# A hybrid block's second stage on one Trainium2 core: the next chunk's products, convolution and delta moved into this chunk's scan loop

## Chip, cores and metric

One core of a Trainium2 chip. The metric is the device time of one launch in microseconds (us); the kernel before takes 3812.79 us, the median of 3 runs (3812.38 to 3813.08).

## The reference

Three blocks follow each other on `x` of 2 sequences x 2048 tokens x 512 channels, viewed as needed: (1) an RWKV attention block with a recurrence over time; (2) a feed-forward block, and a Mamba block around which it stands; all with LayerNorm ahead and a residual behind. What matters here is the Mamba block and the feed-forward block (gate, up and down weights gathered from a table of 16 values, `silu(gate) * up`, then down):

```python
proj = einsum('blh,eh->ble', hidden, in_proj_w)        # 512 -> x (1024) and gate (1024)
x, gate = proj[..., :1024], proj[..., 1024:]
u = silu(conv1d(x, 4 taps, causal, per channel) + conv_b)
ssm_p = einsum('bld,rd->blr', u, x_proj_w)             # 128 (low rank of delta) + 16 (B) + 16 (C)
delta = softplus(einsum('blr,dr->bld', dt_lr, dt_proj_w) + dt_proj_b)
def step(h, xs):                                       # 16 states per channel
    h = h * exp(d_t[..., None] * A) + (d_t * u_t)[..., None] * B_t[:, None, :]
    return h, einsum('bdn,bn->bd', h, C_t)
y = (scan(step) + u * D_param) * silu(gate)
return einsum('bld,hd->blh', y, out_proj_w)
```

## The kernel before

The 4096 tokens are cut into 16 chunks of 256 (`NC = 16`, `CH = 256`). A first stage (to about 731 us) does the RWKV block; the change leaves it alone. The second stage runs feed-forward and Mamba over the chunks. Everything is written out by hand per engine: each engine has its own `step(i)` for chunk i, and semaphores join them, so that an engine's order is the order of its code.

In `step(i)` there are two parts. A **head**, in which TensorE (PE) has already made x of chunk i in PSUM (`first_product`, two halves of four 128-channel tiles in `W[0]` and `W[1]`), ScalarE (ACT) copies it to SBUF with room for three older tokens (`xext`) and starts `U` (`taps`), VectorE (DVE) adds the three other taps (`conv`, L1259), ACT applies silu (`smooth`, L944), PE multiplies by `x_proj_w` (L1137 and L1141) and by `dt_proj_w` into the eight PSUM tiles `D` (L1147), and delta follows by pairs of tiles: `D + bias` capped (DVE L1285, "below"), exp and ln on ACT (`soft`, L970 and L972), the maximum (DVE L1292), and `U * delta` (DVE L1297). Then a **scan loop** of 64 steps, one per state n and pair j of tiles (e = 4n + j): ACT computes `exp(delta * A)` into the pair's tiles of `D` (L1007), GpSimd (POOL) `dBu = U*delta * B` (L866), DVE two scans over the 256 tokens in place in `D` (L1308) and the product with C (L1327 or L1330), and POOL (three pairs of four, L879) or DVE (the fourth, L1339) adds it into `yacc`. ACT's exponentials of step e wait until the product of step e-4 is there, since they overwrite its tiles.

Inside the loop, at steps given by `places`, ACT and DVE serve two feed-forward blocks that PE runs meanwhile: one of a chunk ahead (`early`, F1) and one of the chunk before (`late`, F2). Each is a LayerNorm (`stats` and `shift` on DVE, `norm` on ACT), a transpose on PE (`turn`), its copy to SBUF (`evac`), six pieces of gate and up products with silu (ACT) and `gated` (DVE), the down products (L1096), and a residual (`resid`). PE also multiplies the gate half of `in_proj_w` (L1159) and projects the finished chunk (`project`, L1114). `gate_y` (L1237) closes the chunk. `W[0]` and `W[1]` are the only PSUM besides `D`, and all of this shares them. ACT must hold the right function table: `ACT_TABLE_LOAD` stands in its stream wherever the next function needs another one.

## Time and profile before

| | |
|---|---|
| median of 3 runs | 3812.79 us |
| the profiled execution's own time | 3813.42 us |
| its span in the trace | 3811.6 us |
| granted TensorE clock, mean | 0.942 of full |
| busy share of the span | PE 87%, PEld 62%, DVE 86%, ACT 65%, POOL 64% |
| first stage, second stage | 0 to about 731 us, about 731 to 3811.6 us |

The span is the time from the first to the last instruction of the one profiled execution; its own time is 1.8 us longer, and the median of the runs is 0.6 us below that. PE is the matrix engine with PEld its weight loads, which overlap it. Busy shares are means over stages with different limits, so the chunks are read one by one in the trace. A float32 matmul is two instructions in the trace.

### The profile page before, as it was taken

The numbers are of one execution on the slowest core, as the hardware profiler recorded it, in microseconds if no ns is written. First come the engines' busy times: TensorE is split into PE (matmuls) and PEld (weight loads), VectorE is DVE, ScalarE is ACT, GpSimd is POOL, SyncE is SP. The second block draws the span as 40 slices with busy tenths as digits, with TensorE's granted clock in tenths as the row PEclk, the third lists the DMA queues.
The fourth block names the chain that finished last, engine by engine and source line by source line (L and its number), as shares of the span: only waits on it lengthen the run. The fifth ranks groups of instructions, "written<-read, shape, count | busy, mean of one in ns | idle before, by whom it ended". The sixth has DMA issues, their size and how long they took to land.

```text
span 3811.6 us, 46308 instructions
## 1 busy us (share of the span) xinstructions
PE 3318.6 (87%) x12672; PEld 2365.7 (62%) x12672; DVE 3286.4 (86%) x6128; ACT 2489.4 (65%) x4790; POOL 2454.7 (64%) x1943
## 2 busy tenths in 40 slices
PE   5888984999999999999999999999999999985738
PEld 4666662666767676767676767666666666663515
DVE  5888883299999998989898989898989898989891
ACT  4777672186767676767676858676767676765650
POOL 0344343086869595959595959595969595957470
PEclk8999997999999999999999999999999999987868
DMA  2222212111111111111111111111111111101010
GB/s 99 65 74 73 76 61 84 61 37 40 30 43 31 42 33 41 39 34 41 34 41 34 41 33 41 34 39 35 40 35 39 35 39 37 47 27 37 20 36 6
DMA packets 119378, 165.36 MB, mean 43 GB/s; under 512 B 8545, under 2 KB 84193, under 8 KB 118625
## 3 DMA queue, kind: packets, MB, share of 16 engines
q1 hardware_dynamic: 119136, 162.63, 15.2%
q8 instruction: 92, 1.51, 0.2%
q14 instruction: 150, 1.22, 0.1%
HBM read 128.39 MB, written 25.69 MB: 40 GB/s over the span
## 4 chain that ended last, share of the span: by engine, by line
POOL 28%; PE 20%; DVE 17%; issue 15%; ACT 2%; DVEq 1%; POOLq 0%; DMA 0%; SPq 0%; ACTq 0%
POOL dBu L866 16%; POOL yacc L879 12%; DVE D L1308 10%; PE W L1064 6%; PE W L1114 5%; PE W L1096 3%; PE W L1137 2%; DVE prod L1327 2%; PE W L1141 2%; DVE D L1330 2%; PE D L1064 1%; DVE U L1259 1%; DVE yacc L1339 1%; ACT L916 1%; DVE hT L1221 1%
## 5 line engine op out<-in xcount | busy, mean ns | idle before, releaser
L1308 DVE TENSOR_TENSOR_SCAN D<-D,hc,dBu 128x256 f32<-128x256 f32 x2048 | 1436.9, 740 | 47.0 <-ACT D L1007 47.0
L866 POOL TENSOR_TENSOR dBu<-U,BC 128x512 f32<-128x512 f32 x1024 | 1294.3, 1275 | 276.4 <-DMA BC<-bc_scratch 200.3
L1064 PE MATMUL W<-nT,wffn 128*128 128x256 f32 x5632 | 1241.6, 382 | 47.2 <-ACT nT L905 32.6
L1064 PEld LDWEIGHTS W<-nT,wffn 128*128 128x128 f32 x5632 | 1058.8, 189 | 230.6 <-ACT nT L905 37.5
L1007 ACT ACTIVATE D<-delta,A 128x256 f32<-128x256 f32 x2048 | 891.7, 468 | 425.7 <-DVE yacc L1339 404.8
L879 POOL TENSOR_TENSOR yacc<-yacc,prod 128x512 f32<-128x512 f32 x736 | 933.9, 1269 | 263.0 <-DVE prod L1327 258.5
L1096 PE MATMUL W<-wffn,hT 128*128 128x512 f32 (+1 forms) x1408 | 642.0, 613 | 41.5 <-DVE hT L1221 41.5
L1096 PEld LDWEIGHTS W<-wffn,hT 128*128 128x128 f32 (+1 forms) x1408 | 273.8, 197 | 373.4 <-issue 323.8
L1327 DVE TENSOR_TENSOR prod<-D,BC 128x512 f32<-128x512 f32 x736 | 494.6, 672 | 0.0
L1064 PE MATMUL W<-nT,win 128*128 128x256 f32 x2048 | 453.9, 383 | 33.7 <-ACT nT L905 33.7
L1064 PEld LDWEIGHTS W<-nT,win 128*128 128x128 f32 x2048 | 391.4, 192 | 106.4 <-ACT nT L905 44.9
L450 PE MATMUL rvkP<-xnT,wr 128*128 128x256 f32 x1536 | 348.8, 387 | 31.3 <-ACT kk L328 16.0
L450 PEld LDWEIGHTS rvkP<-xnT,wr 128*128 128x128 f32 x1536 | 296.7, 194 | 83.2 <-ACT kk L328 17.8
L1114 PE MATMUL W<-wo,sgm 128*128 128x512 f32 x512 | 229.4, 602 | 65.3 <-DVE sgm L1237 65.3
L1007 ACT ACT_TABLE_LOAD x212 | 272.0, 1283 | 3.8
L848 POOL TENSOR_TENSOR rstd<-veps,mhalf 128x2 f32<-128x2 f32 x48 | 33.6, 699 | 349.5 <-DVE veps L1207 349.5
L995 ACT ACTIVATE hc<-D 128x2 f32<-128x2 f32 x736 | 117.3, 159 | 191.2 <-DVE prod L1327 190.7
L916 ACT ACT_TABLE_LOAD x182 | 233.5, 1283 | 3.3
L429 PE MATMUL trP<-wo,yT 128*128 128x512 f32 x256 | 140.5, 711 | 90.1 <-POOL yT L272 55.5
L1114 PEld LDWEIGHTS W<-wo,sgm 128*128 128x128 f32 x512 | 97.0, 192 | 182.5 <-issue 181.8
L1221 DVE TENSOR_TENSOR hT<-nrm,W 128x512 f32<-128x512 f32 x192 | 121.5, 633 | 95.9 <-ACT nrm L916 95.9
L1339 DVE TENSOR_TENSOR yacc<-D,yacc 128x512 f32<-128x512 f32 x288 | 193.5, 672 | 2.3
(118 smaller groups left out, 3212.0 us busy)
## 6 DMA issues: line engine op xcount, KB each, us to landing
BC<-bc_scratch SPq DMA_DIRECT2D x256, 256.0 KB, 4.6
XM<-x_scratch SPq DMA_DIRECT2D x29, 512.0 KB, 4.9
X<-x_scratch SPq DMA_DIRECT2D x17, 512.0 KB, 3.6
ix<-idx SPq DMA_DIRECT2D x33, 255.0 KB, 2.9
X<-x SPq DMA_DIRECT2D x16, 512.0 KB, 3.4
XR<-x SPq DMA_DIRECT2D x16, 512.0 KB, 3.4
x_scratch<-XR SPq DMA_DIRECT2D x16, 512.0 KB, 3.7
out<-X SPq DMA_DIRECT2D x16, 512.0 KB, 2.8
```

Of the source, the lines that this page charges most:

```text
L450: last = T_.matmul(rvkP[u % 3][:, m % 2, :], wr[:, k, part * H + m * P:part * H + (m + 1) * P], xnT[sf][:, k, :], start=(k == 0), stop=(k ...
L866: nc.gpsimd.tensor_tensor(dBu[e % 4][:], U[:, 2 * j:2 * j + 2, :], BC[slot][:, 0:1, :].to_broadcast([P, 2, CH]), ALU.mult).then_inc(s_dBu, 1)
L879: nc.gpsimd.tensor_tensor(y, y, prod[r % 2][:], ALU.add).then_inc(s_acc, 1)
L916: N_.activation(nrm[0:r[0][1], p % 2, 0:w], W[(side + p) % 2][0:r[0][1], 0:len(r), :].rearrange("p a t -> p (a t)"), ACT.Silu).then_inc(f_ ...
L1007: N_.activation(D[:, m, :], delta[:, m, :], ACT.Exp, scale=A[:, m, n:n + 1]).then_inc(s_dA, 1)
L1064: last = T_.matmul(dst, lhsT, rhs, start=(n == 0), stop=(n == len(terms) - 1))
L1096: return T_.matmul(o[:, t, :], hT[0:r, k, t * P:(t + 1) * P], wd[0:r, k, :], start=(k == 0), stop=(k == MI - 1))
L1114: last = T_.matmul(o[:, t, :], sgm[:, k, t * P:(t + 1) * P], wo[:, k, :], start=(k == 0), stop=(k == ME - 1))
L1221: V.tensor_tensor(hT[0:n, 2 * p:2 * p + w, :], nrm[0:n, p % 2, 0:w * CH].rearrange("p (a t) -> p a t", a=w), W[(side + p) % 2][0:n, 2:2 + ...
L1308: V.tensor_tensor_scan(D[:, m, :], D[:, m, :], dBu[e % 4][:, m % 2, :], hc[:, n, m:m + 1], ALU.mult, ALU.add).then_inc(s_scan, 1)
L1327: V.tensor_tensor(prod[r % 2][:], h_, c_, ALU.mult).then_inc(s_prod, 1)
L1339: V.tensor_tensor(yacc[:, pair, :], D[:, pair, :], yacc[:, pair, :], ALU.add).then_inc(s_prod, 1)
```

## The change

A head no longer stands between two scan loops. While chunk i is scanned, x of chunk i+1 is made (`first`), its convolution (`conv`, now reading x directly out of PSUM `W`), silus and `x_proj` are done, and the last steps of the loop are mixed with chunk i+1's delta, pair by pair (`delta_proj`, `below`, `soft`, `to_delta`). So that x can be read in place, `xext` goes; the three first tokens of a tile get their missing taps from a small tensor `edge`, which POOL makes out of the last three tokens of the chunk before (`tail`). `U * delta` goes to a tensor of its own (`dU`), the transposed rows `nT` get two buffers, the output residual is done in two halves, the list of places is new, and the last two chunks also give POOL three of four sums. The explicit load of the table that holds both exp and ln (L960) is taken out. The normalised rows for `first` are made one chunk earlier, which saves one reload of a row buffer per chunk. The core of the difference:

```diff
-xext = [buf(ctx, f"xext{s}", [2, CH + KC - 1]) for s in range(2)]
-cc = buf(ctx, "cc", [ME, KC - 1])
+nT = [buf(ctx, f"nT{s}", [KH, CH]) for s in range(2)]
+dU = buf(ctx, "dU", [ME, CH])
+tail = buf(ctx, "tail", [ME, KC - 1])
+edge = buf(ctx, "edge", [ME, KC - 1])
+term = buf(ctx, "term", [ME, KC - 1])
...
+    if i + 2 < NC:
+        stat = [(norm_no(*early(i)), 1), (norm_no(*late(i)), 8), (norm_no("M", i + 2), 41)]
+        return dict(stat=stat, early=(1, 3), late=(8, 10), m=(NEVER, NEVER), m2=(41, 43), out=(4, 6),
+                    norm=5, gate=(9, 12), evac=18, silu=(21, 24, 27, 29, 32, 34), res=38,
+                    norm2=36, evac2=39, silu2=(44, 46, 49, 52, 54, 56), res2=NEVER, norm_m=NEVER, evac_m=NEVER, norm_m2=58, evac_m2=NEVER,
+                    taps=(14, 17), conv=(12, 14), smooth=(21, 21, 24, 24), low=61, bc=63)
...
-            pe.wait_ge(s_prod, NE * i)
-            pe.wait_ge(s_ha, pool_sums(i))
-            pe.wait_ge(m_dtl, i + 1)
-            for m in range(ME):
-                last = chain(D[:, m, :], [(wdt[:, m * P:(m + 1) * P], dtl[:])])
-                if m % 2:
-                    last.then_inc(m_dp, 1)
-            if back:
-                project(i - 1, 0, FILL)
-                project(i - 1, 1)
+        def delta_proj(k):
+            pe.wait_ge(m_dtl, k + 1)
+            for j in range(4):
+                if k:
+                    e = NE - 4 + j
+                    pe.wait_ge(s_prod, NE * (k - 1) + e + 1)
+                    pe.wait_ge(s_ha, pool_sums(k - 1) + upto(e + 1))
+                for m in (2 * j, 2 * j + 1):
+                    last = T_.matmul(D[:, m, :], wdt[:, m * P:(m + 1) * P], dtl[:], start=True, stop=True)
+                last.then_inc(m_dp, 1)
+            if low is not None:
+                x_proj(low, 1 - side)
+            for k in range(MI):
+                if k == TURN_AT and then is not None:
+                    if low is not None:
+                        pe.wait_ge(m_bcS, low + 1)
+                    turn(then, 1 - side)
+            for m in range(4):
+                last = gate(i, m)
+            last.then_inc(m_g, 1)
+            if i:
+                project(i - 1)
+            for m in range(4, ME):
+                if i and m % 2 == 0:
+                    pe.wait_ge(m_res, 2 * (i - 1) + m // 2 - 1)
+                last = gate(i, m)
+            last.then_inc(m_g, 1)
+            if i + 1 < NC:
+                pe.wait_ge(m_sg, 2 * i + 1)
+                first(i + 1, 0)
+                pe.wait_ge(m_sg, 2 * i + 2)
+                first(i + 1, 1)
+                pe.wait_ge(m_tail, 2 * i + 5)
+                free = (m_tail, 2 * i + 6)
+            if i + 2 < NC:
+                turn(norm_no(*early(i)), 0)
+                ffn(ffn_no(*early(i)), norm_no(*early(i)), i % 2, 0, free, L)
+                ffn(F, L, i % 2, 1, (f_res, F), norm_no("M", i + 2), i + 1)
+            if i + 1 < NC:
+                delta_proj(i + 1)
...
-                N_.activation(xext[q % 2][:, :, KC - 1:], src[:, a:a + 2, :], ACT.Copy).then_inc(m_ext, 1)
-                act.wait_ge(s_dBu, NE * i)
-            N_.preload_act_table_set("natural_log_exp_and_others")
-            skip(0)
-            skip(1)
-            soft(0)
-            soft(1)
+        def taps(k, q):
+            act.wait_ge(m_x, 2 * k + q // 2 + 1)
+            act.wait_ge(m_du, 4 * k)
+            for h in range(2):
+                m = 2 * q + h
+                N_.activation(U[:, m, :], W[q // 2][:, m % 4, :], ACT.Identity, bias=cb[:, m:m + 1],
+                              scale=cw[:, m, KC - 1:KC]).then_inc(m_tap, 1)
+        def smooth(k, q):
+            act.wait_ge(m_edge, 2 * k + q // 2 + 1)
+            N_.activation(U[:, 2 * q:2 * q + 2, :], U[:, 2 * q:2 * q + 2, :], ACT.Silu).then_inc(m_u, 1)
+                for m in (2 * j, 2 * j + 1):
+                    N_.activation(D[:, m, :], delta[:, m, :], ACT.Exp, scale=A[:, m, n:n + 1]).then_inc(s_dA, 1)
+                if e == 0:
+                    soft(i, 3)
+                if e < 4:
+                    skip(i, e)
+                    if i + 1 < NC and e == at["taps"][h]:
+                        taps(i + 1, 2 * h)
+                        taps(i + 1, 2 * h + 1)
+                if f1 and e == at["evac"]:
+                    evac(norm_no(*early(i)), i % 2, 0)
+                if i + 1 < NC and e == at["low"]:
+                    low_rank(i + 1, 1 - side_late(i))
+                if i + 1 < NC and e == at["bc"]:
+                    b_and_c(i + 1, 1 - side_late(i))
+            if 0 < i < NC - 2:
+                evac(norm_no("M", i + 2), i % 2, 0)
+            for j in range(4):
+                save(i, NE - 4 + j)
+                if i + 1 < NC and j < 3:
+                    soft(i + 1, j)
...
+        def edges(k):
+            pool.wait_ge(m_tail, 2 * k + 2)
+            pool.wait_ge(m_edge, 2 * k)
+            nc.gpsimd.tensor_tensor(edge[:], tail[:], cw[:, :, 0:1].to_broadcast([P, ME, KC - 1]), ALU.mult).then_inc(m_term, 1)
+            for d in (1, 2):
+                pool.wait_ge(m_term, 5 * k + 2 * d - 1)
+                w = KC - 1 - d
+                nc.gpsimd.tensor_tensor(term[:, :, 0:w], tail[:, :, d:KC - 1], cw[:, :, d:d + 1].to_broadcast([P, ME, w]),
+                                        ALU.mult).then_inc(m_term, 1)
+                pool.wait_ge(m_term, 5 * k + 2 * d)
+                nc.gpsimd.tensor_tensor(edge[:, :, 0:w], edge[:, :, 0:w], term[:, :, 0:w], ALU.add).then_inc(m_term, 1)
...
-            V.tensor_copy(x_[:, :, 0:KC - 1], cq).then_inc(m_in, 1)
-                    V.scalar_tensor_tensor(U[:, m, :], x_[:, h, k:k + CH], cw[:, m, k:k + 1], U[:, m, :],
-                                           ALU.mult, ALU.add).then_inc(m_conv, 1)
-            V.tensor_scalar(cq, x_[:, :, CH:CH + KC - 1], keep[:, bass.ds(i + 1, 1)], None, ALU.mult).then_inc(m_cc, 1)
+        def conv(k, q):
+            dve.wait_ge(m_tap, ME * k + 2 * q + 2)
+            for d in range(KC - 1):
+                for h in range(2):
+                    m = 2 * q + h
+                    if d:
+                        dve.wait_ge(m_conv, 24 * k + 6 * q + 2 * (d - 1) + h + 1)
+                    V.scalar_tensor_tensor(U[:, m, KC - 1 - d:CH], W[q // 2][:, m % 4, 0:CH - KC + 1 + d], cw[:, m, d:d + 1],
+                                           U[:, m, KC - 1 - d:CH], ALU.mult, ALU.add).then_inc(m_conv, 1)
+        def ends(k, h):
+            half = slice(4 * h, 4 * h + 4)
+            dve.wait_ge(m_term, 5 * (k + 1))
+            V.tensor_scalar(tail[:, half, :], W[h][:, :, CH - KC + 1:CH], keep[:, k + 1:k + 2], None, ALU.mult).then_inc(m_tail, 1)
+            dve.wait_ge(m_conv, 24 * k + 12 * (h + 1))
+            V.tensor_tensor(U[:, half, 0:KC - 1], U[:, half, 0:KC - 1], edge[:, half, :], ALU.add).then_inc(m_edge, 1)
...
-            V.tensor_scalar(hc[:], hc[:], keep[:, bass.ds(i, 1)], None, ALU.mult).then_inc(s_hz, 1)
-            dve.wait_ge(s_scan, 2 * NE * i)
+        def below(k, j):
+            if k:
+                dve.wait_ge(s_scan, 2 * NE * (k - 1) + 2 * (NE - 3 + j))
+        def to_delta(k, j):
+            pair = slice(2 * j, 2 * j + 2)
+            V.tensor_tensor(dU[:, pair, :], U[:, pair, :], delta[:, pair, :], ALU.mult).then_inc(m_du, 1)
+                if e == 1:
+                    to_delta(i, 3)
+                if i and more and e >= NE - 2 and e <= NE:
+                    below(i + 1, e - NE + 2)
+                if i and more and e >= NE:
+                    to_delta(i + 1, e - NE)
+                for h in range(2):
+                    if more and e == at["conv"][h]:
+                        conv(i + 1, 2 * h)
+                        conv(i + 1, 2 * h + 1)
+                        ends(i + 1, h)
+            gate_y(i)
+            if more:
+                to_delta(i + 1, 2)
+                below(i + 1, 3)
```

Three places in the order of the instructions. First VectorE, end of the scan loop and start of the next chunk's (chunk 1 to 2; `D` holds first the delta projection, then the scan's factors and states). Before, the whole head stands between two loops:

```order
L1279 TENSOR_SCALAR hc<-hc,keep 128x128
L1285 TENSOR_SCALAR dBu<-D,bdt 128x256 x8
L1292 SCALAR_TENSOR_TENSOR delta<-D,bdt,dBu 128x256 x2
L1297 TENSOR_TENSOR U<-U,delta 128x512
L1292 SCALAR_TENSOR_TENSOR delta<-D,bdt,dBu 128x256 x2
L1297 TENSOR_TENSOR U<-U,delta 128x512
```

After (a scan is printed as SCALAR_TENSOR_TENSOR):

```order
L1331 SCALAR_TENSOR_TENSOR D<-D,hc,dBu 128x256 x2
L1351 TENSOR_TENSOR prod<-D,BC 128x512
L1312 TENSOR_SCALAR dBu<-D,bdt 128x256 x2
L1331 SCALAR_TENSOR_TENSOR D<-D,hc,dBu 128x256 x2
L1351 TENSOR_TENSOR prod<-D,BC 128x512
L1312 TENSOR_SCALAR dBu<-D,bdt 128x256 x2
L1339 COPY hc<-D 128x2
L1354 TENSOR_TENSOR D<-D,BC 128x512
L1312 TENSOR_SCALAR dBu<-D,bdt 128x256 x2
L1321 SCALAR_TENSOR_TENSOR delta<-D,bdt,dBu 128x256 x2
L1324 TENSOR_TENSOR dU<-U,delta 128x512
```

One block of eight has become three pairs that alternate with the last scans. Second ScalarE at the same place, where delta's exp (L970) and ln (L972) stand. Before:

```order
L960 ACT_TABLE_LOAD
L965 ACTIVATE yacc<-U,dsk 128x256 x4
L970 ACTIVATE dBu<-dBu 128x512
L972 ACTIVATE dBu<-dBu 128x512
L970 ACTIVATE dBu<-dBu 128x512
L972 ACTIVATE dBu<-dBu 128x512
```

After (L964 is the exp, L966 the ln, L973 the copy that saves a pair's last state):

```order
L906 ACTIVATE nT<-W 128x1024
L973 ACTIVATE hc<-D 128x2
L964 ACTIVATE dBu<-dBu 128x512
L966 ACT_TABLE_LOAD
L966 ACTIVATE dBu<-dBu 128x512
L973 ACTIVATE hc<-D 128x2
L964 ACT_TABLE_LOAD
L964 ACTIVATE dBu<-dBu 128x512
L966 ACT_TABLE_LOAD
L966 ACTIVATE dBu<-dBu 128x512
L973 ACTIVATE hc<-D 128x2
```

Every change between exp and ln now has a load of its own, and each save stands behind the exp and ln of the pair before. Third TensorE over one chunk, from the end of the second feed-forward block to the middle of the next. Before:

```order
L1064 MATMUL W<-nT,win 128x256 x32
L1137 MATMUL W<-U,wx 128x256 x2
L1141 MATMUL W<-U,wx 32x256 x2
L1137 MATMUL W<-U,wx 128x256 x2
L1141 MATMUL W<-U,wx 32x256 x2
L1114 MATMUL W<-wo,sgm 128x512 x4
```

After:

```order
L1071 MATMUL W<-U,wx 128x256 x8
L1071 MATMUL W<-U,wx 32x256 x8
L1123 MATMUL W<-wffn,hT 128x512 x6
L1079 MATMUL W<-ident,nrm 128x128 x8
L1123 MATMUL W<-wffn,hT 128x512 x5
L1099 MATMUL D<-dtl,wdt 128x256 x8
L1071 MATMUL W<-nT,win 128x256 x16
L1146 MATMUL W<-wo,sgm 128x512 x16
L1071 MATMUL W<-nT,win 128x256 x48
L1079 MATMUL W<-ident,nrm 128x128 x8
L1071 MATMUL W<-nT,wffn 128x256 x80
```

The `x_proj` products have moved into the second feed-forward block; the delta projection follows its last product; 48 products in a row (the second half of the gate, then x of the next chunk) stand ahead of the transpose of the first feed-forward block.

## Rows read from the trace of the kernel before

**Rows 1.** Windows by stage: length, busy time and instructions of each engine, granted clock

```profile
core 0: us, PE busy (x) PEld busy (x) DVE busy (x) ACT busy (x) POOL busy (x), PEclk, DMA share, GB/s
731.00:923.37 192.37, 178.23 (x711) 133.41 (x712) 170.30 (x314) 134.80 (x269) 140.65 (x116) 0.96 0.14 37
923.37:3341.49 2418.12, 2269.85 (x8738) 1609.73 (x8737) 2254.44 (x4095) 1713.31 (x3420) 1830.83 (x1495) 0.98 0.14 38
3341.49:3811.60 470.11, 307.28 (x1079) 208.82 (x1077) 362.74 (x676) 221.74 (x456) 240.87 (x196) 0.81 0.11 24
```

**Rows 2.** Windows inside one chunk: its head, then its scan loop

```profile
2039.94:2074.03 34.09, 28.85 (x90) 15.38 (x89) 26.63 (x63) 22.71 (x42) 5.79 (x5) 0.95 0.09 25
2074.03:2225.33 151.30, 145.14 (x586) 108.24 (x585) 146.65 (x254) 109.08 (x223) 134.85 (x110) 0.99 0.15 41
```

**Rows 3.** Waits in two chunks, 2039.94 to 2412.00: who waited, total, times, longest

```profile
PE W L1137 <- ACT U L944: 10.5, 2, 5.2
DVE dBu L1285 <- PE D L1064: 8.5, 2, 4.8
DVE D L1308 <- ACT D L1007: 6.7, 4, 1.9
```

**Rows 4.** Timeline of PE, one chunk: start, length, instructions, idle before

```profile
2026.36 14.08 PE L1064 MATMUL W<-nT,win 128*128 128x256 f32 x64 [1.39 <-ACT nT L905]
...
2050.27 1.05 PE L1141 MATMUL W<-U,wx 128*32 128x256 f32 x4
...
2062.32 10.46 PE L1114 MATMUL W<-wo,sgm 128*128 128x512 f32 x24
```

**Rows 5.** Timeline of PE, a feed-forward block without waits

```profile
850.48 38.15 PE L1064 MATMUL W<-nT,wffn 128*128 128x256 f32 x176
...
903.93 4.46 PE L1096 MATMUL W<-wffn,hT 128*128 128x512 f32 x10
```

**Rows 6.** Timeline of PE in the last chunks, behind long waits

```profile
3401.20 41.27 PE L1064 MATMUL W<-nT,wffn 128*128 128x256 f32 x176 [5.16 <-ACT nT L905]
...
3480.62 16.64 PE L1064 MATMUL W<-nT,win 128*128 128x256 f32 x64 [12.97 <-ACT nT L905]
```

**Rows 7.** Timeline of DVE, the same point of the loop, four steps apart

```profile
2141.77 1.38 DVE L1308 TENSOR_TENSOR_SCAN D<-D,hc,dBu 128x256 f32<-128x256 f32 x2
...
2149.97 1.39 DVE L1308 TENSOR_TENSOR_SCAN D<-D,hc,dBu 128x256 f32<-128x256 f32 x2
```

**Rows 8.** Timeline of DVE: statistics, residual, gate, convolution, below, delta

```profile
2006.54 1.27 DVE L1202 BATCH_NORM_STATS2 bnst<-XM 128x6 f32<-128x512 f32 x2
...
2009.13 1.39 DVE L1308 TENSOR_TENSOR_SCAN D<-D,hc,dBu 128x256 f32<-128x256 f32 x2
...
2026.86 1.20 DVE L1227 TENSOR_TENSOR X<-W,X 128x1024 f32<-128x1024 f32 x1
...
2039.94 2.36 DVE L1237 TENSOR_TENSOR sgm<-yacc,sgm 128x1024 f32<-128x1024 f32 x2
...
2042.50 2.46 DVE L1259 SCALAR_TENSOR_TENSOR U<-xext,cw,U 128x256 f32<-128x256 f32 x6
...
2060.01 3.39 DVE L1285 TENSOR_SCALAR dBu<-D,bdt 128x256 f32<-128x256 f32 x8 [3.70 <-PE D L1064]
...
2065.10 0.87 DVE L1292 SCALAR_TENSOR_TENSOR delta<-D,bdt,dBu 128x256 f32<-128x256 f32 x2
...
2067.18 0.86 DVE L1292 SCALAR_TENSOR_TENSOR delta<-D,bdt,dBu 128x256 f32<-128x256 f32 x2
```

**Rows 9.** Timeline of ACT: a table load, exponentials, delta's exp and ln

```profile
1995.21 1.28 ACT L916 ACT_TABLE_LOAD   x1
1996.50 0.60 ACT L916 ACTIVATE nrm<-W 128x512 f32<-128x512 f32 x1
...
1998.47 0.87 ACT L1007 ACTIVATE D<-delta,A 128x256 f32<-128x256 f32 x2
...
2062.17 0.61 ACT L970 ACTIVATE dBu<-dBu 128x512 f32<-128x512 f32 x1
2062.82 0.63 ACT L972 ACTIVATE dBu<-dBu 128x512 f32<-128x512 f32 x1
```

782 lines of the change are left out of this document (380 added, 402 removed).

## The prediction, made before the changed kernel ran

> **What bounds the kernel now.** I began with the windows by stage [rows 1]. The twelve columns to read are each engine's busy time: between two gates thirteen chunks take 2418.1 us, 186.0 each, of which PE is busy 174.6, DVE 173.4, POOL 140.8, ACT 131.8. Two engines are nearly full, so no chunk can go below about 175 us with this work, and the idle time that the change can aim at is about 11 to 13 us per chunk. The windows inside a chunk [rows 2] show where it is: the head takes 34.1 us with DVE busy 26.6, the loop 151.3 with DVE busy 146.7. The waits [rows 3] name it: per chunk DVE waits 4.3 us for the delta projection and 3.4 for exponentials at the loop's start, PE 5.2 for the silus. Both engines lose about the same, in the head, and neither is far from the other in the loop.
>
> **The parts, priced.** DVE: one scan step costs 8.20 / 4 = 2.05 us [rows 7]. Statistics with a root cost 2.6 in the loop [rows 8], I take 2.3 as an average with a `veps` that needs no wait; half a residual .65, two gates 2.4, six taps 2.46, below .85 a pair, a pair of delta 2.1 (start to start of 2065.10 and 2067.18) [rows 8]. The trace has no convolution that reads PSUM inside the loop. The nearest row is L1292, also one PSUM and one SBUF source, while POOL works: .43 each against .41 for a tap, so 2.46 stays; the other bound, each of six ops waiting a whole .4 more, would be 9.6 us per chunk. PE: 64 products 14.0, so 7.0 for a half; projection 14.0 (24 in 10.46, eight more at that pace); `x_proj` 8.3 at 1.05 for four [rows 4]; a feed-forward block 57.9 (850.48 to 908.39) [rows 5]. ACT: table load 1.28, the next function starts 1.29 behind it; a pair of exponentials .87, exp .61, ln .63 [rows 9].
>
> The Trainium skill ("ScalarE: Activation LUTs", What ACT_TABLE_LOAD costs) puts a switch of sets at 1283 ns for the load and some 1380 ns of drain. The first half agrees with [rows 9], the second does not show there: the load ends where the next activation starts. By the page the four loads that I find on the path below would cost 5.5 us more per chunk, an estimate of 72 us more in all, and the sum would be about 4265. I go by the row.
>
> **A chunk of the changed kernel, walked through** (time 0: DVE starts scan step 0).
>
> First stretch, DVE. Step 1's exponentials stand on ACT behind exp, load, ln of delta's fourth pair (2.5), a pair of `skip` (.87, as the exponentials), a load (1.28) and themselves (.87): ready at 5.6, where DVE is done with step 0 at 1.3. Wait 4.3. Sixteen steps are 32.8. Put between them: the fourth pair of delta 2.1, two statistics 4.6, two shifts 1.4, residual halves 1.3, convolution 9.8, `ends` 1.6 (estimate, twice a small op and one that follows it). `taps` for the second half stand at ACT's step 17, which needs the product of step 13; DVE makes that just before it wants to convolve at step 14, so it waits for save, exponentials and one pair of taps: 2.1. Sum 32.8 + 20.8 + 6.4 = 60.0. Only then is the product of step 14 there, which ACT's step 18 needs, and only in step 18 stands `evac` (exponentials, save, 1.0 for the copy): 62.
>
> Meanwhile PE: gate 7, projection 14, gate 7, x 14, with small waits for the residual halves (at 19 and 24) and the gate's silu (36), done at 43; the transpose follows the first tail at 45. It then has nothing until 62: **PE idles some 16 us**, where before it waits 1.15. This is the term that decides.
>
> Second stretch, PE. Two feed-forward blocks 115.8 and `x_proj` 8.3, plus 2.8 for a restart: in [rows 6] the same 176 instructions take 41.27 behind a wait of 5.2 instead of 38.15, and 64 take 16.64 behind 13.0 instead of 14.08. So PE ends at 62 + 126.9 = 188.9. DVE needs for steps 16 to 61 only 94.3 + about 12, so it waits for PE, first at the residual of step 38 and again at the end; ACT's step 61 waits for `x_proj`. What was DVE's lack in the first stretch is now PE's, and the other way round: the two no longer work at the same time.
>
> Third stretch, the border. `evac` and the save of step 60 are done before PE's last product, so pair 0 of delta: PE .95, below .85, with hand-overs 2.0. Pair 1 waits for exp, load, ln (2.6), the save behind them (.25), PE (.95 at 2.4 GHz, about 2.0 if the granted clock is at its lower level of 1.2 GHz; the head has .95 of full on average [rows 2], the last two chunks with their long waits .81 [rows 1]), below .85: 4.9 to 5.9. Pair 2 the same. Then DVE alone: delta pair 2.1, sum .6, pair 2.1, gates 2.4, residual 1.2, pair 2.1, below .85 = 11.3. Sum 23 to 25, so 23.7. The next step 0 starts at 212.6.
>
> That is 26.6 us more than 186.0 per chunk, for thirteen chunks 346 us.
>
> **The ends.** Chunk 0: ahead of its loop, `x_proj` no longer runs between the silus (6 us) and three exp/ln pairs have loads (2): +8. Its loop does all of chunk 1's head after the second feed-forward block: from the loop's start 23 to `evac`, 118.6 for the two blocks, then first products 7, statistics and taps, convolutions with the steps between them, silus, `x_proj` behind a cold start 11, two rounds of exp/ln: about 72. That is 214, before 182 (192.4 from 731, of which the prologue is 44, plus the head of 34) [rows 1, 2]: +32, together +40. The last two chunks and the tail take 470.1 us from the gate of chunk 13 [rows 1], 435 from the next loop's start. After: chunk 14 about 187 (DVE alone: 131 for the steps, 34 between, the waits above and 5 for PE), chunk 15 154 (no convolution, no delta), tail 89.5 as before: 430, -5.
>
> Sum: 3811.6 + 346 + 40 - 5 = 4192.6 span, 1.8 more for the execution's own time. The median of the runs is .6 below the profiled one: **4194**, and 4193 is what I write.
>
> What costs nothing: POOL's five `edges` ops lie under its slack (140.8 of 212). The fewer row loads and the queue's new order don't reach the path: the copies of B and C have 30 us more than before. POOL's sums in the last chunks replace DVE's.
>
> The Trainium skill ("SBUF — State Buffer", on the shared port pair) says that a DVE op with two SBUF inputs is shut out while POOL reads SBUF, for that whole instruction. By that rule the convolution out of PSUM is free of POOL, while `U * delta` and the `edge` sums, now inside the loop, are not; the row for the pair of delta (2.1) was taken while POOL worked and has it in, and for the two `edge` sums it would be an estimate of 2 us per chunk, 26 in the sum.
>
> **The rivals.**
> *PE is not held at `evac`.* If DVE were in its step 15 by about 45 (my stretch too long by 16), PE would run through: 44 for gate to transpose, 124 for blocks and `x_proj`, and from its last product to the gate of the next chunk the border up to DVE's last sum, 2.0 + 9.8 + 2.7 + 1 plus 4 for restarts = 19.5. That is 187.6 per chunk, +21 in thirteen, with the ends 3868. For it: [rows 7] is a calm stretch. Against: each inserted op has a row. Chance .06; between this and the forecast (192 to 206 per chunk, 3925 to 4105) .10.
> *The border costs nothing (the other side: faster).* One mechanism: exp and ln need no load between them because one table set holds both, and PE is again ahead of DVE. Without four loads the cycle that DVE alone sets (its 173.4 of work, +2 in the loop, waits 4.3 + 2.1 + 6 less 5.1) is 182.7, -43 in thirteen, +35 at the ends: 3805; with 180 per chunk 3770. It decides below 183.3. Against: the built order has every load, and [rows 9] their price. The Trainium skill (same page, Table sets) says that one set holds both functions, so the loads could be spared, but not by this program. Chance .06.
> *It does what it aims at nowhere:* gain and loss within .2%, period 182.7 to 183.9: .02.
> *More than forecast.* PE at 1.2 GHz also in the gate and projection behind the border, or convolutions at the upper bound of 9.6 more: 4320. That stretch ends before `evac`, so a slow start there is swallowed by the wait. Chance .06.
>
> **The numbers.** The forecast's own case has .70. Its range: border 23 to 25, first stretch 58 to 65, small waits within the blocks 0 to 3: 208 to 217 per chunk, 4134 to 4251. To hold 8 in 10 the range takes in the upper part of the case below: 4050 to 4275. A difference under .2% (8 us) is what a measurement of this kernel can't tell from none. Faster .06, same .02, slower .92.
>
> **What would show it.** PE with a wait of some 16 us per chunk ahead of the first feed-forward block's 176 products, for ACT's copy to `nT`; DVE waiting at the residual of step 38 and at the first `below` (8 us or more each); 5.6 from step 0 to step 1; three pairs of below 5 us apart; periods of about 212 with PE busy near 175. Wrong if PE's wait at `evac` is small, if loads hide behind other waits, or if DVE waits for nothing and the period is near 186.

## The result, and the profile after

| | before | changed |
|---|---|---|
| median of the runs | 3812.93 us (3812.38 to 3814.51) | 4182.23 us (4179.56 to 4182.91) |
| profiled span | 3811.6 us | 4181.0 us |
| mean granted clock of TensorE | 0.942 of full speed | 0.891 of full speed |

The changed kernel is slower by 9.7%: ratio 1.0966, 95% interval 1.0947 to 1.0985. The prediction said 4193 us, slower with a chance of .92.

First the windows by stage, which answer to [rows 1], and then the three stretches of one chunk that the prediction walked through: from DVE's scan step 0 to the end of ACT's copy to `nT`, to PE's last product of the second feed-forward block, and to the next step 0.

```profile
core 0: us, PE busy (x) PEld busy (x) DVE busy (x) ACT busy (x) POOL busy (x), PEclk, DMA share, GB/s
731.00:972.37 241.37, 187.56 (x737) 142.22 (x738) 183.02 (x344) 151.89 (x284) 144.30 (x127) 0.87 0.11 28
972.37:3741.84 2769.47, 2323.37 (x8767) 1664.02 (x8766) 2273.66 (x4055) 1796.79 (x3462) 1854.28 (x1561) 0.90 0.12 30
3741.84:4181.00 439.16, 289.96 (x1022) 201.12 (x1020) 324.90 (x560) 219.23 (x467) 279.55 (x231) 0.81 0.12 27
...
2055.59:2117.64 62.05, 43.90 (x164) 31.45 (x163) 52.87 (x106) 37.34 (x77) 38.45 (x37) 0.86 0.13 36
2117.64:2243.22 125.58, 124.79 (x488) 90.27 (x489) 106.21 (x181) 87.47 (x172) 98.81 (x81) 0.99 0.14 30
2243.22:2267.22 24.00, 9.30 (x22) 5.87 (x21) 15.48 (x26) 12.47 (x16) 5.33 (x4) 0.59 0.05 20
```

In thirteen chunks DVE is busy 2273.7 us, where it was 2254.4, and PE 2323.4, where it was 2269.9: hardly more work in 351 us more time, and PE's 53 us more come with a granted clock of .90 instead of .98. Read the columns of the three stretches against each other. In the first PE lacks 18 us and DVE 9, in the second PE 1 and DVE 19, in the third PE 15 and DVE 9. The chunk from gate to gate, 2048.82 to 2260.45, lasts 211.6 us. Its waits (who waited, total, times, longest) answer to [rows 3]:

```profile
DVE dBu L1312 <- PE D L1099: 16.8, 3, 9.6
...
PE W L1071 <- ACT nT L906: 14.5, 1, 14.5
PE D L1099 <- ACT hc L973: 7.6, 2, 3.8
DVE XM L1267 <- PE W L1123: 7.0, 1, 7.0
...
DVE D L1331 <- ACT D L990: 4.9, 2, 4.3
...
DVE U L1294 <- ACT U L935: 3.9, 2, 2.1
```

The timeline of PE over the same chunk shows where those waits stand; [rows 5] and [rows 6] have the 176 products without a wait and behind one.

```profile
2077.25 13.98 PE L1071 MATMUL W<-nT,win 128*128 128x256 f32 x64
2092.94 7.17 PE L1071 MATMUL W<-nT,win 128*128 128x256 f32 x32 [1.71 <-ACT sgm L1002]
...
2102.06 1.09 PE L1079 MATMUL W<-ident,nrm 128*128 128x128 f32 x8 [1.95 <-DVE tail L1301]
2117.64 39.95 PE L1071 MATMUL W<-nT,wffn 128*128 128x256 f32 x176 [14.49 <-ACT nT L906]
...
2238.93 4.46 PE L1123 MATMUL W<-wffn,hT 128*128 128x512 f32 x10
2243.22 1.03 PE L1099 MATMUL D<-dtl,wdt 128*128 128x256 f32 x4
2248.05 2.05 PE L1099 MATMUL D<-dtl,wdt 128*128 128x256 f32 x4 [3.79 <-ACT hc L973]
2253.89 2.04 PE L1099 MATMUL D<-dtl,wdt 128*128 128x256 f32 x4 [3.80 <-ACT hc L973]
```

And the border on DVE, then on ACT: three pairs of `below`, each behind PE's product, each 5.84 us after the one before, and on ACT a load of 1.28 us between every `exp` and `ln` (the first pair is shown).

```profile
2244.36 0.88 DVE L1312 TENSOR_SCALAR dBu<-D,bdt 128x256 f32<-128x256 f32 x2 [9.62 <-PE D L1099]
...
2250.20 0.88 DVE L1312 TENSOR_SCALAR dBu<-D,bdt 128x256 f32<-128x256 f32 x2 [3.08 <-PE D L1099]
...
2256.04 0.88 DVE L1312 TENSOR_SCALAR dBu<-D,bdt 128x256 f32<-128x256 f32 x2 [4.09 <-PE D L1099]
...
2260.45 3.42 DVE L1277 TENSOR_TENSOR sgm<-yacc,sgm 128x1024 f32<-128x1024 f32 x2
...
2267.22 1.39 DVE L1331 TENSOR_TENSOR_SCAN D<-D,hc,dBu 128x256 f32<-128x256 f32 x2
2272.93 1.40 DVE L1331 TENSOR_TENSOR_SCAN D<-D,hc,dBu 128x256 f32<-128x256 f32 x2 [4.32 <-ACT D L990]
```

```profile
2245.27 0.63 ACT L964 ACTIVATE dBu<-dBu 128x512 f32<-128x512 f32 x1 [5.06 <-DVE dBu L1312]
2245.92 1.28 ACT L966 ACT_TABLE_LOAD   x1
2247.21 0.63 ACT L966 ACTIVATE dBu<-dBu 128x512 f32<-128x512 f32 x1
2247.75 0.15 ACT L973 ACTIVATE hc<-D 128x2 f32<-128x2 f32 x1
```

The `hc` copy of .15 us is what PE's next product waits for, and it stands behind exp, load and ln. The rows tell where the time stands, not yet what sets it: in this kernel each engine waits for another one somewhere.

### The profile page after: what moved, and what is told of

The parts are those of the page before. It is cut to its first block, busy times and chain, and to the rows that moved or that the text cites. A ratio compares the mean times of both kernels' runs of the same rounds, so it can differ in the third digit from the quotient of the medians.

```text
span 4181.0 us, 46642 instructions
## 1 busy us (share of the span) xinstructions
PE 3364.3 (80%) x12672; PEld 2421.8 (58%) x12672; DVE 3280.5 (78%) x6002; ACT 2587.5 (62%) x4858; POOL 2519.9 (60%) x2055
## 3 DMA queue, kind: packets, MB, share of 16 engines
q1 hardware_dynamic: 115328, 155.29, 13.8%
## 4 chain that ended last, share of the span: by engine, by line
PE 43%; DVE 17%; issue 12%; ACT 6%; POOL 6%; DVEq 0%; POOLq 0%; DMA 0%; SPq 0%; ACTq 0%
PE W L1071 27%; PE W L1123 13%; DVE D L1331 5%; DVE U L1294 4%; POOL dBu L861 3%; POOL yacc L875 2%; PE D L1099 2%; ACT D L990 2%; DVE prod L1351 1%; DVE sgm L1277 1%; ACT L966 1%; DVE yacc L1364 1%; DVE dBu L1312 1%; DVE bnst L1242 1%; DVE delta L1321 1%
## 5 line engine op out<-in xcount | busy, mean ns | idle before, releaser
L861 POOL TENSOR_TENSOR dBu<-dU,BC 128x512 f32<-128x512 f32 x1024 | 1305.1, 1285 | 419.4 <-DVE dU L1324 368.3
L875 POOL TENSOR_TENSOR yacc<-yacc,prod 128x512 f32<-128x512 f32 x768 | 975.5, 1270 | 657.0 <-DVE prod L1351 655.3
L1071 PEld LDWEIGHTS W<-nT,wffn 128*128 128x128 f32 x5632 | 1078.0, 192 | 408.2 <-ACT nT L906 219.7
L1123 PE MATMUL W<-wffn,hT 128*128 128x512 f32 (+1 forms) x1408 | 618.1, 593 | 1.1 <-DVE hT L1261 1.1
L1071 PE MATMUL W<-nT,win 128*128 128x256 f32 x2048 | 497.9, 407 | 80.0 <-issue 51.4
L1351 DVE TENSOR_TENSOR prod<-D,BC 128x512 f32<-128x512 f32 x768 | 515.9, 672 | 1.4 <-issue 1.4
L1071 PEld LDWEIGHTS W<-nT,win 128*128 128x128 f32 x2048 | 418.6, 206 | 167.9 <-issue 68.4
L973 ACT ACTIVATE hc<-D 128x2 f32<-128x2 f32 x768 | 121.9, 159 | 289.3 <-DVE prod L1351 289.3
L1099 PE MATMUL D<-dtl,wdt 128*128 128x256 f32 x256 | 112.3, 587 | 194.6 <-ACT hc L973 150.1
L1312 DVE TENSOR_SCALAR dBu<-D,bdt 128x256 f32<-128x256 f32 x128 | 55.9, 479 | 251.6 <-PE D L1099 251.6
L1294 DVE SCALAR_TENSOR_TENSOR U<-W,cw,U 128x253 f32<-128x253 f32 (+2 forms) x384 | 152.5, 473 | 74.1 <-ACT U L935 74.1
```

The lines of the kernel that those rows point to most:

```text
L861: nc.gpsimd.tensor_tensor(dBu[e % 4][:], dU[:, 2 * j:2 * j + 2, :], BC[g % 3][:, 0:1, :].to_broadcast([P, 2, CH]), ALU.mult).then_inc(s_dB ...
L875: nc.gpsimd.tensor_tensor(y, y, prod[r % 2][:], ALU.add).then_inc(s_acc, 1)
L1071: last = T_.matmul(dst, lhsT, rhs, start=(n == 0), stop=(n == len(terms) - 1))
L1099: last = T_.matmul(D[:, m, :], wdt[:, m * P:(m + 1) * P], dtl[:], start=True, stop=True)
L1123: return T_.matmul(o[:, t, :], hT[0:r, k, t * P:(t + 1) * P], wd[0:r, k, :], start=(k == 0), stop=(k == MI - 1))
L1294: V.scalar_tensor_tensor(U[:, m, KC - 1 - d:CH], W[q // 2][:, m % 4, 0:CH - KC + 1 + d], cw[:, m, d:d + 1], U[:, m, KC - 1 - d:CH], ALU.mu ...
```

## Experiments

Two theories at the start. **A, the places:** the loss is made by three queues' order. `evac` stands at step 18, so PE has nothing to do while DVE catches up; then DVE has too little while PE catches up; and in the border the table loads and the order of the `hc` copies let four engines work one after the other. **B, the work:** DVE, PE and ACT have more to do, or work slower, once the second stage is inside the loop, and what order it has matters little. Their forecasts for each run are in its expectation. "Period" below is the mean distance of the gates of chunks 1 to 13 in the profiled execution: 186.0 us before, 211.7 changed.

| kernel | us (range) | ratio to before, interval | period |
|---|---|---|---|
| changed | 4182.2 (4179.6 to 4182.9) | 1.0966 (1.0947 to 1.0985) | 211.7 |
| evac at 20 | 4246.7 (4245.8 to 4247.8) | 1.1135 (1.1117 to 1.1154) | 216.6 |
| evac at 15 | 4122.1 (4119.6 to 4124.7) | 1.0812 (1.0794 to 1.0830) | 207.2 |
| one table set | 4119.2 (4111.0 to 4120.9) | 1.0804 (1.0786 to 1.0822) | 207.1 |
| saves first | 4095.6 (4094.1 to 4097.9) | 1.0742 (1.0724 to 1.0760) | 205.8 |
| all three (evac at 15) | 3995.2 (3994.6 to 3999.4) | 1.0476 (1.0459 to 1.0494) | 199.0 |
| + gate in the border | 3989.1 (3987.6 to 3991.2) | 1.0462 (1.0445 to 1.0480) | 198.3 |
| + all places moved | 3813.7 (3807.0 to 3824.8) | 1.0007 (0.9998 to 1.0017) | 184.8 |
| + border on DVE | 3724.6 (3721.1 to 3736.1) | 0.9769 (0.9755 to 0.9782) | 179.8 |
| + chunk 0 | 3715.2 (3713.0 to 3725.1) | 0.9750 (0.9736 to 0.9763) | 178.0 |
| convolution at 9 | 3752.2 (3750.5 to 3752.7) | 0.9837 (0.9823 to 0.9850) | 180.9 |
| + evac at 12 | 3721.2 (3720.1 to 3722.4) | 0.9758 (0.9745 to 0.9771) | 178.8 |

**Evac at 20, evac at 15.** The place of one copy, two steps later and three earlier, in the row of places of chunks 1 to 13.

```diff
-                            norm=5, gate=(9, 12), evac=18, silu=(21, 24, 27, 29, 32, 34), res=38,
+                            norm=5, gate=(9, 12), evac=20, silu=(21, 24, 27, 29, 32, 34), res=38,
```

> evac is moved from 18 to 20 in every chunk's row, the rest as in the changed kernel. Theory A (between evac and the silus everything runs one after the other: VectorE's steps up to evac, ScalarE's normalization of 1.0 us, TensorE's products, VectorE again): each of the two steps that now lie ahead of evac adds its 2.15 us to the first stretch and takes them from the second only where VectorE waits there anyway; the period of 211.6 us grows by about 4.3 us, over 13 chunks 56 us, 4238 us (4225 to 4250). Theory B (the place of evac doesn't matter, since TensorE's own work between the gates sets the period): 4182 us within 8 us.

> One number changed: ACT copies the first feed-forward block's transposed rows at its step 15 instead of 18. Theory A (three stretches in series: DVE up to that copy, PE for the two blocks, then the border): PE's wait of 14.5 us ahead of the 176 products shrinks to about 3, of which some 4.5 come back as a wait for the first silu, which still stands at step 21; period 211.6 less 7.3 = 204.3, time about 4088 us (4078 to 4100). Theory B (the loss is work and contention, not order: PE is busy 178.0 per chunk instead of 174.6, and what is taken off one wait comes back at the next): no change, 4175 to 4185.

Two steps later cost 64.5 us, 5.0 per chunk; three earlier gave 60. B's "no change" fails both times. A held for the first (4246.7 in its 4225 to 4250) and missed the second (4122.1, outside its 4078 to 4100). With evac at 15 PE's waits before and in the first block read as follows.

```profile
2080.76 16.11 PE L1071 MATMUL W<-nT,wffn 128*128 128x256 f32 x64 [2.73 <-ACT nT L906]
2101.30 26.13 PE L1071 MATMUL W<-nT,wffn 128*128 128x256 f32 x112 [4.43 <-DVE hT L1261]
2127.86 14.86 PE L1123 MATMUL W<-wffn,hT 128*128 128x512 f32 x34 [0.43 <-DVE hT L1261]
```

The wait of 14.5 us has become 2.73 + 4.43 + .43: the next link, the silus that I had left at step 21, shows up behind the one that was moved. The gain is 4.5 per chunk and not the 7.3 of the expectation. The difference is a second restart: 64 products in 16.11 us, where 64 take 13.98 in the middle of work, and 112 in 26.13, where 112 of the second block take 24.44 behind a wait of .79. Together the 176 take 42.2 us, 2.3 more than the 39.95 of the changed kernel; the waits fell by 6.9.

**One table set, saves first.** The border's queue on ACT: in the first the set that holds exp and ln is asked for once, ahead of it; in the second the copies of the end columns go ahead of the exp and ln that PE's next product doesn't need.

```diff
+                    if i + 1 < NC:
+                        N_.preload_act_table_set("natural_log_exp_and_others")
                     for j in range(4):
                         save(i, NE - 4 + j)
```

> The explicit load of the table set that holds both exp and ln is put back, once per chunk, ahead of the border: 105 loads fewer. Theory A: four loads of 1.28 lie on the path per chunk (two at the border, two between scan step 0 and step 1): wait before step 1 from 4.3 to 1.8, pairs of below 4.6 apart instead of 5.8; period -5.1, with the ends about 4109 us (4095 to 4118). Theory B: the loads lie under PE's and DVE's waits and only ACT's busy time falls (135 us over the run): 4175 to 4185. The skill's 2.66 us a switch would give 10.6 per chunk: about 4035.

```diff
-                    for j in range(4):
-                        save(i, NE - 4 + j)
-                        if i + 1 < NC and j < 3:
-                            soft(i + 1, j)
+                    save(i, NE - 4)
+                    save(i, NE - 3)
+                    if i + 1 < NC:
+                        soft(i + 1, 0)
+                    save(i, NE - 2)
+                    save(i, NE - 1)
+                    if i + 1 < NC:
+                        soft(i + 1, 1)
+                        soft(i + 1, 2)
```

> Only the order on ACT at the border: the save of step 61 stands ahead of the exp and ln of pair 0, that of step 62 ahead of pair 1's. Theory A: the wait for the second pair (3.1 us) goes, of the third's 4.1 some 1.6 stay: period -5.6, time about 4105 us (4092 to 4120). Theory B (the border is set by DVE's and PE's own work or by the table loads): under 20 us in all.

Measured: 63 us where A said 73 (1 us outside its range), and 87 where it said 77 (in its range); B fails in both. In the second of the two the three pairs of `below` stand 5.84 us from first to third on DVE's timeline, and not 11.68, which is the whole gain of 5.8 per chunk:

```profile
2005.82 0.88 DVE L1317 TENSOR_SCALAR dBu<-D,bdt 128x256 f32<-128x256 f32 x2 [9.61 <-PE D L1104]
...
2008.50 0.86 DVE L1317 TENSOR_SCALAR dBu<-D,bdt 128x256 f32<-128x256 f32 x2
...
2011.66 0.88 DVE L1317 TENSOR_SCALAR dBu<-D,bdt 128x256 f32<-128x256 f32 x2 [1.43 <-PE D L1104]
```

With one set, DVE's waits for the second and third pair fall from 3.08 and 4.09 to 1.17 and 2.81, and the one for step 1 from 4.32 to 1.61, 5.9 us together. Only 4.5 of it arrives. Part of what is given back is in a row that neither theory had, the load from memory of the rows for the statistics, which was never late before:

```profile
2031.00 1.40 DVE L1333 TENSOR_TENSOR_SCAN D<-D,hc,dBu 128x256 f32<-128x256 f32 x2 [1.61 <-ACT D L990]
...
2036.59 1.29 DVE L1244 BATCH_NORM_STATS2 bnst<-XM 128x6 f32<-128x512 f32 x2 [2.10 <-DMA XM<-x_scratch]
```

**All three together.**

> The three together. Theory A, serial stretches: the gains add, 7.3 + 2.6 + 6.3 = 16.2 per chunk, less 1 to 2 because with a shorter DVE stretch the copy at step 15 finds PE's transpose only just done: period 195.4 to 197, about 3975 us (3955 to 3995). Theory B (each wait has another one right behind it): clearly less than the sum of the three single gains.

One by one the edits gave 60, 63 and 87 us, 210 in sum; in one kernel they give 187, so 23 are lost. That is .2 us outside A's range, and the loss that B wanted is there, though small. Most of it lies in the border, where two of the edits shorten the same stretch: from the first pair of `below` to the third it is 11.68 us in the changed kernel, 8.49 with one table set, 5.84 with the saves first, and 4.37 with all three. The two single gains are 9.0 us, the joint one is 7.3, and 1.7 us in 13 chunks are 22 us.

```profile
1967.53 0.88 DVE L1319 TENSOR_SCALAR dBu<-D,bdt 128x256 f32<-128x256 f32 x2 [9.62 <-PE D L1106]
...
1971.90 0.88 DVE L1319 TENSOR_SCALAR dBu<-D,bdt 128x256 f32<-128x256 f32 x2
```

**The gate in the border.** PE computes the first half of the next chunk's gate between the delta products.

```diff
                        last.then_inc(m_dp, 1)
+                        if k and j:
...
+                            for m in ((0,), (1, 2), (3,))[j - 1]:
+                                last = gate(k, m)
```

> This is the kernel with all three edits together (evac at 15, one table set, saves ahead of the softs; 3995 us), and in it the gate's first 32 products of the next chunk stand on TensorE between the delta products of the border (8 after the second pair, 16 after the third, 8 after the fourth), where TensorE waited 3 to 4 us three times. Theory A (the places in the table set when VectorE and ScalarE want the products after the gate, so products that are done earlier are only waited behind later): TensorE's 10.2 us for the gate leave the stretch after the border, but the wait at evac grows by as much, and the border itself gains or loses under 1 us: 3995 us (3980 to 4010). Theory B (TensorE's order is what is late after the border): up to 7 us in each of 13 chunks, 3904 us.

6 us, as A said. Filling an engine's idle time gives nothing while another engine's place in the queue says when the next stage starts. PE now waits 3.14 and 3.26 us for residuals of DVE and 4.89 for the silus.

**All places moved.**

```diff
-                return dict(stat=stat, early=(1, 3), late=(8, 10), m=(NEVER, NEVER), m2=(41, 43), out=(4, 6),
-                            norm=5, gate=(9, 12), evac=18, silu=(21, 24, 27, 29, 32, 34), res=38,
...
-                            taps=(14, 17), conv=(12, 14), smooth=(21, 21, 24, 24), low=61, bc=63)
+                return dict(stat=stat, early=(5, 7), late=(26, 28), m=(NEVER, NEVER), m2=(53, 55), out=(3, 4),
+                            norm=10, gate=(6, 9), evac=13, silu=(16, 18, 21, 24, 26, 28), res=33,
...
+                            taps=(12, 14), conv=(10, 12), smooth=(18, 18, 21, 21), low=58, bc=60)
...
-                        if e == 0:
+                        if e == 1:
                             soft(i, 3)
-                        if e < 4:
+                            skip(i, 0)
+                        if 0 < e < 4:
                             skip(i, e)
...
+                N_.preload_act_table_set("natural_log_exp_and_others")
                 for j in range(3):
                     soft(0, j)
```

> The gate within the border as in the run before, the saves and the table set too, the exponentials of step 1 ahead of the fourth pair's soft, and all places of chunks 1 to 15 moved: the first feed-forward's evac at 13 instead of 18 with its silus from step 16, the second's evac at 34 instead of 39 with its silus from 38, conv at 10 and 12, statistics and turns behind them. Theory A (the loss of the changed kernel is where the places put TensorE's waits, not its amount of work): walking one chunk's rows with these places, TensorE waits about 2 us at each evac and VectorE about 4 us in the border, a period of 178.5 to 182 us instead of the 186.0 of the kernel before and the 211.6 of the changed one; with chunk 0 as it is, 3745 us (3720 to 3800). Theory B (the second stage within the scan's loop adds waits wherever it is put, since ScalarE's table loads and the exchange between engines remain): no period under that of the three edits together, 198.8 us by some 8 at most, 190 us and above: 3880 us and over.

3813.7 us: 175 less, by the order of the same work, and the time of the kernel before. Most of the edit is numbers in the table, for the last two chunks too. With them exp and ln of the fourth pair went behind step 1's exponentials, and one table load ahead of chunk 0's pairs; what each part gave isn't separated. B, which said 3880 and over, is out as far as the big loss goes. A's own range of 3720 to 3800 was missed too, and the trace shows a thing that neither had. Windows from gate to gate, the last two of five chunks in a row and the first two of the seven after them:

```profile
1701.19:1881.86 180.67, 171.07 (x674) 124.12 (x673) 175.11 (x313) 128.75 (x259) 142.87 (x120) 0.99 0.15 36
1881.86:2062.51 180.65, 171.06 (x674) 124.11 (x673) 175.07 (x313) 128.73 (x259) 142.84 (x120) 0.99 0.14 36
2062.51:2250.21 187.70, 177.57 (x674) 127.80 (x673) 175.66 (x312) 128.81 (x259) 142.77 (x120) 0.95 0.14 35
2250.21:2437.94 187.73, 177.60 (x674) 127.80 (x673) 175.90 (x314) 128.82 (x259) 142.79 (x120) 0.95 0.17 35
```

The same instructions of the same program, 180.7 to 181.0 us each up to there and 187.7 each from there on. DVE, ACT and POOL have the same busy time to within 1 us; PE has 6.5 more, and its granted clock is .95 instead of .99. What is slower lies in the first half of the chunk: the projection's 32 products take 13.97 us in the one and 16.92 in the other, behind the same wait of 3.14 us, and the first block's 176 take 38.25 and 40.49, behind the same wait of 1.11. From the second block on the groups take the same time to .01 us, up to the next border. The forecast of 178.5 to 182 was right for the first kind. The profiled execution, the fastest of the ten at 3807.0 us, is 62 us above the 3745 of A: seven chunks of the second kind are 49 of them, and chunk 1 the rest: 194.9, since its deltas still come behind the gate.

**The border on DVE.** ACT copies the first end column before the copy of the turned norm; the residual goes into DVE's first wait; the gate's first half goes where only its own pairs must be final.

```diff
+                    save(i, NE - 4)
                     if 0 < i < NC - 2:
                         evac(norm_no("M", i + 2), i % 2, 0)
...
-                    save(i, NE - 4)
                     save(i, NE - 3)
...
+                        if e == NE - 2 and at["res2"] > NE + 1:
+                            resid(ffn_no(*late(i)), late_rows, side_late(i))
                         if i and more and e >= NE - 2 and e <= NE:
                             below(i + 1, e - NE + 2)
+                        if i and more and e == NE:
+                            gate_y(i, (0,))
```

> On top of the retimed kernel (3814 us): ScalarE copies out the first of the last four end columns before the 1.0 us copy of the turned norm and the 1.28 us table load that stood ahead of it; the residual of 1.2 us moves into VectorE's first wait of the border; the gate's first half moves to where only its own pairs are final. Theory A (VectorE's queue from the first of these waits to the next chunk's first step is the chain that ends last): the wait of 3.15 us for the first delta product falls to about 0.6, the gate saves 0.5 to 1 of its 3.42 us, so 3.1 to 3.6 us less in each of 13 chunks: 3770 us (3755 to 3790). Theory B (TensorE, with 171 us of work at a granted clock of 0.99 and 178 at 0.95, is the limit of a chunk): VectorE's time turns into waits for TensorE, 3800 us and over.

**Chunk 0.**

```diff
-                            norm2=24, evac2=27, silu2=(32, 35, 38, 40, 43, 44), res2=50, norm_m=46, evac_m=50, norm_m2=57, evac_m2=61,
-                            taps=(55, 58), conv=(54, 57), smooth=(62, 62, 62, 62), low=63, bc=63)
+                            norm2=24, evac2=27, silu2=(32, 35, 38, 40, 43, 44), res2=50, norm_m=46, evac_m=50, norm_m2=57, evac_m2=59,
+                            taps=(55, 57), conv=(54, 56), smooth=(60, 60, 60, 60), low=62, bc=63)
```

> As the run before, and in chunk 0 the convolution's second half at step 56 instead of 57, the norm's copy at 59 instead of 61, the silus of U at 60 instead of 62, the low rank's copy at 62. Theory A (VectorE's 5.6 us for the first delta product behind chunk 0's gate comes from the silus, which were the last link of TensorE's wait of 6.6 us): the projections end some 5 to 7 us earlier and all behind them too, 6 us less than the run before. Theory B (TensorE is late there by its own work): within 2 us of the run before.

The border gave 89 us where I had written 44, below A's range, and with both edits the kernel is 2.5% faster than the one before. The border's three moves were made together, so what each gave isn't separated. After the edit in chunk 0 the median is 9 us lower where I had written 6, but that this edit made the difference is not shown: in the profiled executions PE starts chunk 0's projection 2.1 us earlier (978.55 against 980.61), not 5 to 7, and the gate of chunk 1 comes .9 earlier (1152.09 against 1153.00). The rest lies in chunks whose code is the same, and the runs of the two kernels overlap. Why the border gave twice its price is in the windows of the last of the two, again from gate to gate:

```profile
1861.70:2039.93 178.23, 171.66 (x673) 124.04 (x672) 173.98 (x312) 128.95 (x258) 142.81 (x120) 0.99 0.17 36
2039.93:2221.91 181.98, 175.66 (x673) 127.03 (x672) 174.09 (x313) 128.94 (x258) 142.85 (x120) 0.96 0.15 36
2221.91:2398.75 176.84, 170.00 (x673) 122.75 (x672) 174.18 (x314) 128.87 (x258) 142.85 (x120) 1.00 0.16 37
```

PE's one wait of 3.9 us in the border is now four of 1.50, 1.30, .27 and .83, the one of 3.14 ahead of the projection is gone, and the projection's 32 products take 13.97 us behind every border of the loop, in both kernels. Before these edits seven of twelve chunks took 187.7 us; now two of twelve take 182 and the others 178.4 at most. (In the border run itself, whose profiled execution was its slowest at 3736.1, five of twelve take 182.) The long waits were paid for twice, by their length and by the clock behind them, and I had counted them once.

**Convolution at 9, then evac at 12.** What is left is one wait of PE ahead of the first block. Moving what it waits for, one step earlier, with the first half's taps at ACT's step 11 instead of 12 (the 14 that the expectation names stood there before):

```diff
-                            taps=(12, 14), conv=(10, 12), smooth=(18, 18, 21, 21), low=58, bc=60)
+                            taps=(11, 14), conv=(9, 12), smooth=(18, 18, 21, 21), low=58, bc=60)
```

> As the kernel with chunk 0's new places (3715 us), with the convolution's first half at step 9 instead of 10 and its second half's taps at 14 instead of 12 in chunks 1 to 15. In that kernel TensorE waits 1.57 to 1.83 us for the tail that ends the first half and then 1.11 us for the turned norm, once in a chunk; in some chunks (182.0 us) the granted clock of the next 17 us is 0.73 to 0.82, in others (176.6 to 176.8 us) it stays 1.00. Theory A (that wait is what lets the clock fall, and TensorE is the limit of the chunk behind it): the wait for the tail is gone, all chunks take 175 to 177 us, and the sum is 3690 us (3680 to 3700). Theory B (the limit is VectorE's queue, 174.1 us of work a chunk, and the clock falls for other reasons): TensorE waits elsewhere instead, chunks of 182 us remain: 3715 us within 8 us.

37 us slower: both theories missed the time, though PE does wait elsewhere instead, as B said. The wait for the tail fell to .61, and the next one grew from 1.11 to 2.99, since ACT's copy now stood behind a save that waits for DVE's convolution. On PE's timeline:

```profile
2099.20 0.98 PE L1088 MATMUL W<-ident,nrm 128*128 128x128 f32 x7 [0.61 <-DVE tail L1322]
...
2103.28 39.94 PE L1080 MATMUL W<-nT,wffn 128*128 128x256 f32 x176 [2.99 <-ACT nT L906]
```

> As the run before (convolution's first half at step 9, 3752 us), with evac at 12 instead of 13. In that run the tail came 1 us earlier (TensorE waited 0.61 us for it), but ScalarE then stood behind a save of step 9, which waited 5.1 us for VectorE's convolution, so the turned norm came 3 us late and the granted clock fell. Theory A (only the place of the copy was wrong): the copy goes ahead of that save, TensorE waits 0.6 and 1.1 us, less than in the kernel with the convolution at 10, and the time is 3700 us (3688 to 3715). Theory B (the earlier convolution itself costs, by the 1.29 us that VectorE waits for its taps): 3730 us and over.

31 us came back, as that cause says, but not the 20 more that A wanted; 3721 lies between the two theories: PE's two waits are .57 and 1.11 as forecast, and a third of 1.52 us, for the second half's tail, stands behind 32 products.

```profile
2089.76 1.09 PE L1088 MATMUL W<-ident,nrm 128*128 128x128 f32 x8 [0.57 <-DVE tail L1322]
2091.97 7.17 PE L1080 MATMUL W<-nT,wffn 128*128 128x256 f32 x32 [1.11 <-ACT nT L906]
2100.66 31.37 PE L1080 MATMUL W<-nT,wffn 128*128 128x256 f32 x144 [1.52 <-DVE tail L1322]
```

The kernel with the convolution at 10 keeps the lowest median, 3715.2 us; its runs (3713.0 to 3725.1) and those of this one (3720.1 to 3722.4) overlap, so which of the two is faster is not shown.

## Why the prediction was right, point by point

It said 4193 and 4182 came. Counted between the starts of chunk 1's and chunk 14's loops, the middle costs 333 us more (2752.3 against 2419.1), predicted 346; up to there 38.7, predicted 40; from there on 2.5 less, predicted 5 less. 333.2 + 38.7 - 2.5 = 369.4, the difference of the spans. Of the 38.7, 10.0 are there when chunk 0's loop starts (785.39 against 775.42; predicted 8) and 28.7 come behind it (predicted 32).

The signs that it named came, two of them weaker: DVE waits 7.0 us for the residual of step 38 where 8 or more was written, and PE is busy 178.0 us of a chunk, not near 175, at a granted clock of .90. PE's wait at `evac`, DVE's 9.6 at the first `below`, 5.7 from step 0 to step 1, the pairs 5.84 apart and the period of 211.6 are as written.

**First stretch, 62.** Measured 62.05, with the wait of 4.3 at step 1 (4.32) and the 2.1 before the second convolution (2.14) in their places; a wait of 1.79 before the first was not in my list, and the pair of delta at 2.1 was too dear (1.5 from 2256.84 to 2258.34). `ends`, .22 us each time where I had 1.6 for both, was too dear too. That such errors leave 62.05 against 62 is in part luck. The pair's row had been taken where `U * delta` ran beside POOL and took 1.15 us; in the changed kernel's border it takes .69 beside none (the first line is of the kernel before, the second of the changed one):

```profile
2066.10 1.15 DVE L1297 TENSOR_TENSOR U<-U,delta 128x512 f32<-128x512 f32 x1
...
2257.74 0.69 DVE L1324 TENSOR_TENSOR dU<-U,delta 128x512 f32<-128x512 f32 x1
```

The convolution from PSUM takes 4.77 for two pairs, so the lower bound held.

**PE idles some 16 us at `evac`.** 14.49, since PE was done a little later than walked. That this term decides was tested directly: with `evac` two steps later it is 19.05 in most chunks and the period 5.0 longer, with `evac` three steps earlier it is 2.73 and the period 4.5 shorter.

**Second stretch, 126.9.** 125.6: the 176 products behind the wait take 39.95, 1.8 more than in [rows 5]; I had taken 2.8 from [rows 6].

**The border, 23.7.** 24.0, by errors that cancel. The pairs come 5.84 apart (the upper end of my 4.9 to 5.9, with PE's four products at 2.05 us and a granted clock of .59 over the border). The two gates take 3.42 instead of the 2.36 of [rows 8]. Against these two stand the three pairs of delta, at 1.5 each instead of 2.1. The gates overlap POOL's product, which takes 2.17 there instead of 1.27:

```profile
2260.62 2.17 POOL L861 TENSOR_TENSOR dBu<-dU,BC 128x512 f32<-128x512 f32 x1 [0.78 <-DVE dU L1324]
```

The Trainium skill ("SBUF — State Buffer", on the shared port pair) says that a DVE op with two SBUF inputs and a POOL op that reads SBUF shut each other out, and that the one that starts first keeps the ports for its whole length. I had cited it for the two `edge` sums and overlooked the gate, which is the row that agrees. The sums can't say: they take .16 us each, but no POOL op runs beside one of them in any chunk of this trace. In the kernel with chunk 0's new places the halves of the gate stand apart and take 1.21 and 1.22; there the second starts .17 us ahead of POOL's product, and only POOL's is long, 2.19.

**The price of a table load.** 1.28 us and nothing behind it: 2245.92 + 1.28 is 2247.20, and `ln` starts at 2247.21. With the loads gone DVE's waits fell by 5.9 us per chunk, for four loads of 1.28, 5.1 in all. The drain that the Trainium skill names ("ScalarE: Activation LUTs", What ACT_TABLE_LOAD costs) shows in neither: by the page's price the estimate of the sum was 4265, by the row's 4194.

**The rivals.** None came. "The border costs nothing" was priced at 3805 if the loads could go; with the loads gone alone it is 4119, because PE's wait at `evac` stayed (13.8 to 14.5 us). That rival needed both of its conditions, and so did the way to a faster kernel.

## What to carry to other kernels

Two engines with 173 and 175 us of work in a chunk of 186 gain only if both are kept busy at the same time. A stage moved between two others' steps needs its places worked out again for every engine that it touches, as a walk over one chunk, and here the new table, with one exp and ln moved beside it, was worth 175 us. A wait taken away shows the next link at once: forecast the second-longest wait before you price the first. And on TensorE price a wait by its length and by the slow products behind it.
